# Weight splits moved: ScalarE writes the high halves, VectorE the low halves, GpSimd none

## What is computed

```
def _L0_ffn_ref(hidden_states, gate_w, expert_gate_up, expert_down, shared_gate_up, shared_down, shared_gate_vec):
    ...
    def step(acc, ew):
        w_gu, w_d, cw = ew
        h = _silu_mul(x @ w_gu.T, I)
        return (acc + h @ w_d.T * cw[:, None], None)
    ...
x = x + 0.5 * _L0_ffn_ref(_layernorm(x, axis=-1), ...)
x = x + _L0_attn_ref(_layernorm(x, axis=-1), ...)
x = x + 0.5 * _L0_ffn_ref(_layernorm(x, axis=-1), ...)
x = x + 0.5 * _L1_ffn_ref(_layernorm(x, axis=-1), ...)
x = x + _L1_attn_ref(_layernorm(x, axis=-1), ...)
x = x + 0.5 * _L1_ffn_ref(_layernorm(x, axis=-1), ...)
```

## Time and profile before

| | us |
|---|---|
| median of three runs | 1092.97 |
| lowest, highest | 1092.65, 1095.82 |
| span of the profiled execution | 1092.5 |

### The profile page before, as it was taken

One profiled execution on the slowest core, in us unless ns is written; L12 is line 12 of the kernel. 1 busy time (PEld: TensorE's weight loads), 2 busy tenths in 40 slices (PEclk: granted clock), 3 DMA queues, 4 the chain that ended last, 5 costly groups with the idle time before them and its releaser, 6 DMA issues.

```text
span 1092.5 us, 18432 instructions
## 1 busy us (share of the span) xinstructions
PE 1010.5 (92%) x6692; PEld 584.0 (53%) x6692; DVE 800.6 (73%) x1429; ACT 384.8 (35%) x615; POOL 465.1 (43%) x373
## 2 busy tenths in 40 slices
PE   3989999899899899899799999999999999999997
PEld 1546555455555455555356555554455544555554
DVE  6887776967876967878977786466888778885444
ACT  1223223366423356422232332324432344322332
POOL 3646743466523456525466622231342313422222
PEclk8989999999999999999999999999999999999999
DMA  5212310000000000001233100000000000000000
GB/s 172 87 59 88 101 59 1 1 1 1 1 1 1 1 1 2 1 1 53 64 108 102 44 1 1 0 1 1 1 1 1 1 1 1 1 1 20 1 0 19
DMA packets 11814, 27.38 MB, mean 25 GB/s; under 512 B 1720, under 2 KB 4024, under 8 KB 11744
## 3 DMA queue, kind: packets, MB, share of 16 engines
q1 hardware_dynamic: 11744, 26.44, 8.1%
HBM read 25.38 MB, written 1.05 MB: 24 GB/s over the span
## 4 chain that ended last, share of the span: by engine, by line
PE 51%; DVE 28%; issue 10%; POOL 7%; ACT 3%; DMA 1%; SPq 0%; DVEq 0%; POOLq 0%; ACTq 0%
PE ps L719 28%; PE ps L748 12%; DVE hid L935 4%; POOL hlo L515 3%; DVE hid L937 3%; DVE hid L931 3%; PE ps L730 3%; PE ps L861 2%; POOL scr L554 2%; DVE scr L1119 1%; PE ps L795 1%; PE ps L760 1%; DVE combine L1041 1%; DVE scr L1112 1%; DVE picked L1024 1%
## 5 line engine op out<-in xcount | busy, mean ns | idle before, releaser
L515 POOL TENSOR_TENSOR hlo<-hid,hhi 128x512 f16<-128x512 f32 x208 | 252.2, 1212 | 566.5 <-ACT hhi L592 566.5
L719 PE MATMUL ps<-xhi,whi 128*128 128x512 f16 x832 | 319.7, 384 | 26.1 <-DVE hid L931 25.6
L719 PE MATMUL ps<-xhi,wlo 128*128 128x512 f16 x832 | 319.2, 384 | 0.0
L719 PE MATMUL ps<-xlo,whi 128*128 128x512 f16 x832 | 319.1, 384 | 0.0
L592 ACT ACTIVATE hhi<-hid 128x512 f16<-128x512 f32 x208 | 130.9, 629 | 464.9 <-DVE hid L937 464.7
L931 DVE SCALAR_TENSOR_TENSOR hid<-gtanh,ps 128x512 f32<-128x512 f32 x208 | 142.2, 684 | 174.1 <-ACT gtanh L585 159.6
L748 PE MATMUL ps<-whi,hhi 128*128 128x256 f16 (+1 forms) x832 | 227.7, 274 | 0.8 <-POOL hlo L515 0.8
L748 PE MATMUL ps<-whi,hlo 128*128 128x256 f16 (+1 forms) x832 | 227.3, 273 | 0.0
L748 PE MATMUL ps<-wlo,hhi 128*128 128x256 f16 (+1 forms) x832 | 227.1, 273 | 0.0
L935 DVE TENSOR_TENSOR hid<-hid,ps 128x512 f32<-128x512 f32 x208 | 143.0, 687 | 61.0 <-PE ps L730 56.1
L585 ACT ACTIVATE gtanh<-ps 128x512 f32<-128x512 f32 x208 | 123.3, 593 | 104.7 <-PE ps L719 104.4
(11 more groups left out here) (164 smaller groups left out, 927.4 us busy)
## 6 DMA issues: line engine op xcount, KB each, us to landing
stage<-w_in SPq DMA_DIRECT2D x58, 384.0 KB, 3.1
out<-x SPq DMA_DIRECT2D x2, 512.0 KB, 3.1
sel<-sel_in SPq DMA_DIRECT2D x1, 672.0 KB, 7.7
sel<-sel_in SPq DMA_DIRECT2D x2, 288.0 KB, 3.6
x<-x_in SPq DMA_DIRECT2D x4, 128.0 KB, 2.6
x<-x_in SPq DMA_DIRECT2D x1, 512.0 KB, 8.4
const<-const_in SPq DMA_DIRECT2D x1, 128.0 KB, 2.4
rw<-rw_in SPq DMA_DIRECT2D x1, 64.0 KB, 2.2
```

Of the source, the lines that this page charges most:

```text
L515: pool.tensor_tensor(hlo[:, k, :], hid[:, k % 2, :], hhi[:, k, :], ALU.subtract).then_inc(lo_done, 1)
L719: mm = pe.matmul(ps[:, bank, :], w[:, ds(off, P)], a[:, kc, t0:t0 + HN], start=(n == 0), stop=(n == 3 * KC - 1))
```

## The change

ScalarE now writes `whi`, with one activation that copies `stage` times 256 into f16; VectorE writes `wlo` with one fused operation, `stage` * 256 - `whi`, and waits for ScalarE ahead of it (`w_scaled`). `stage` is no longer written in place. GpSimd has no part in a split. The places in the plan stay: on each engine the split stands behind the chunk's own operations. The waits for the load and, in passes 3 and 4, for the old weights' last use, move from VectorE to ScalarE. SyncE's list and TensorE's stay as they were.

```diff
@@ gpsimd
-            def split(j, g, k):
-                pool.wait_ge(w_scaled, g * 2 + 2)
-                pool.tensor_tensor(wlo[:, ds(j * CW, CW)], stage[:, k, :], whi[:, ds(j * CW, CW)],
-                                   ALU.subtract).then_inc(w_split, 1)
...
-                for j, g, _, slot in splits(r, c, k):
-                    split(j, g, slot)
...
-                elif name == "first_weights":
-                    split(n, n, n)
@@ scalar
+            def split(r, j, group, k):
+                act.wait_ge(stage_loaded[k], group * (16 // SLOTS) + 16)
+                if r in (3, 4):
+                    act.wait_ge(down_done, j + (BASE[3] + 1))
+                act.activation(whi[:, ds(j * CW, CW)], stage[:, k, :], ACT.Copy, scale=W_SCALE).then_inc(w_scaled, 1)
...
                 act.activation(hhi[:, k, :], hid[:, k % 2, :], ACT.Copy).then_inc(hi_done, 1)
+                for j, _, group, slot in splits(r, c, k):
+                    split(r, j, group, slot)
...
+                elif name == "first_weights":
+                    split(PRE, n, 0, n)
@@ vector
-            def split(r, j, g, group, k):
-                dve.wait_ge(stage_loaded[k], group * (16 // SLOTS) + 16)
-                if r in (3, 4):
-                    dve.wait_ge(down_done, j + (BASE[3] + 1))
-                dve.tensor_scalar(whi[:, ds(j * CW, CW)], stage[:, k, :], W_SCALE, None, ALU.mult).then_inc(w_scaled, 1)
-                dve.tensor_scalar(stage[:, k, :], stage[:, k, :], W_SCALE, None, ALU.mult).then_inc(w_scaled, 1)
+            def split(j, g, k):
+                dve.wait_ge(w_scaled, g + 1)
+                dve.scalar_tensor_tensor(out=wlo[:, ds(j * CW, CW)], in0=stage[:, k, :], scalar=W_SCALE,
+                                         in1=whi[:, ds(j * CW, CW)], op0=ALU.mult, op1=ALU.subtract).then_inc(w_split, 1)
```

## The result

The changed kernel takes **1127.31 us** (1127.09 to 1130.03, 4 runs) against 1092.81 us (1090.67 to 1095.82, 4 runs) for the kernel before: ratio 1.031, 95% interval 1.0285 to 1.0335. It is slower by 34.5 us. The forecast was 1126.5 us, with a range of 1107 to 1135. The profiled execution is the slowest of the four (1130.03 us, span 1128.2, mean granted clock 0.984); the spans of the other three are 1125.3 to 1125.6 us at 0.987 to 0.988.

The account below looks back on a forecast made before the run. The prediction took TensorE as the bound at 4.12 us a plain chunk, moving to VectorE's wait loop at 4.76. Terms -1.5 + 6.4 + 8.7 + 7.6 + 11.4 + 0.9 = +33.5 us gave 1126.5 us, range 1107 to 1135.

Parts of the forecast that it names:

- start: Before the first chunks: no GpSimd rival for VectorE, router 0.75 us earlier and 0.7 us less blocking, -1.5 us.
- side work, pass 0: Pass 0 chunks with splits beside layer norm and router: later VectorE queue, partly offset by idle time and less blocking, +6.4 us.
- steady, pass 0: Plain split chunks 12 to 27 of pass 0: 15 x 0.64 us, less 0.9 of slack, +8.7 us.
- +0.9: Loop branches, formerly hidden, delay ScalarE by some 0.1 us every fourth steady chunk: +0.9 us in all.
- side work, pass 3: Pass 3 chunks with splits beside other work, up to chunk 13: hidden product comes later by +7.6 us.
- steady, pass 3 and head of 4: Plain split chunks from chunk 13 of pass 3: 18 x 0.64 us, less 0.9 slack, plus 0.8 residual addition, +11.4 us.
- h: The end of the hidden product's last VectorE operation in a chunk; forecast up to 6.4 us later in pass 0, 7.6 in pass 3.
- rival A: No port wait, hlo and the fused operation run side by side: 4.42 us a plain chunk, 1109 us; chance 0.13.
- The ring: Plain chunks: the loop hhi, whi, wlo, L931, L935, L937 sets the pace at 4.76 us against TensorE's 4.12.
- The port: Plain chunks: the fused operation meets GpSimd's hlo at the shared SBUF port and ends 0.82 us behind it.
- The freed port: Side-work chunks: GpSimd's wlo no longer blocks VectorE, saving 1.5 to 2.3 us in four pass 0 chunks.
- rival C: TensorE's gaps cost clock: the lower level in a fifth of 33 steady chunks, about +23 us, 1150 us; chance 0.05.

Follow-up runs that it names:

- run 2: The changed kernel with GpSimd's hlo waiting, in chunks with a split, until VectorE's fused operation is done: 1121.38 us, ratio 1.026 to the kernel before.
- run 5: The changed kernel with GpSimd's hlo cut to 8 of 512 columns in chunks carrying a split, from the fifth chunk on: 1116.33 us, ratio 1.021 to before.
- run 3: The changed kernel with ScalarE's split gone: VectorE writes whi itself, then the fused low half; GpSimd does no splitting: 1087.95 us, ratio 0.9949 to before.
- Run 1: The changed kernel with ScalarE's whi moved from behind hhi to ahead of the wait for the hidden product: 1077.95 us, ratio 0.9874 to before.

## Why the prediction was right

The last operation of the hidden product (L929) in the changed kernel at five chunks of passes 0, 3 and 4:

```profile
91.09 0.69 DVE L929 SCALAR_TENSOR_TENSOR hid<-hid,ps 128x512 f32<-128x512 f32 x1
...
162.87 0.69 DVE L929 SCALAR_TENSOR_TENSOR hid<-hid,ps 128x512 f32<-128x512 f32 x1
...
510.29 0.69 DVE L929 SCALAR_TENSOR_TENSOR hid<-hid,ps 128x512 f32<-128x512 f32 x1
...
570.84 0.69 DVE L929 SCALAR_TENSOR_TENSOR hid<-hid,ps 128x512 f32<-128x512 f32 x1
...
661.49 0.69 DVE L929 SCALAR_TENSOR_TENSOR hid<-hid,ps 128x512 f32<-128x512 f32 x1
```

They are chunks 12 and 27 of pass 0, 3 and 13 of pass 3 and 4 of pass 4. In the kernel before, the first and the fourth are the earlier trace rows, and the other three are:

```profile
149.16 0.69 DVE L937 SCALAR_TENSOR_TENSOR hid<-hid,ps 128x512 f32<-128x512 f32 x1
...
497.08 0.69 DVE L937 SCALAR_TENSOR_TENSOR hid<-hid,ps 128x512 f32<-128x512 f32 x1
...
629.20 0.69 DVE L937 SCALAR_TENSOR_TENSOR hid<-hid,ps 128x512 f32<-128x512 f32 x1
```

Chunk 0 stands at 22.93 us against 25.77, so each term of the sum can be laid beside its measure, within these two executions:

| term | forecast | measured | from |
|---|---|---|---|
| start | -1.5 | -2.8 | 22.93 - 25.77 |
| side work, pass 0 | +6.4 | +6.6 | 91.09 - 87.36 = 3.7, less the start |
| steady, pass 0 | +8.7 and half of +0.9 | +9.1 | 162.87 - 149.16 = 13.7, less 3.7, less 0.9 of slack taken back in chunk 0 of pass 1 |
| side work, pass 3 | +7.6 | +7.2 | 570.84 - 550.48 = 20.4, less 510.29 - 497.08 = 13.2 |
| steady, pass 3 and head of 4 | +11.4 and half of +0.9 | +11.9 | 661.49 - 629.20 = 32.3, less 20.4 |
| everywhere else | 0 | +3.8 | the rest of 35.7 |

The steps between were right too: of the 21 values that the prediction gives for h in the side-work chunks, none is off by more than 0.4 us in pass 0 and 0.5 in pass 3, once the start and the 13.2 us are taken off. What was luck is that the total came so close: the start gained 1.3 us more than forecast and everywhere else lost 3.8 that were not foreseen, which partly offset each other in this execution, and the other three had spans 2.6 to 2.9 us shorter. In the prediction rival A's 10.2 us should read 33 x 0.3 = 9.9, which moves nothing.

**The ring was right to the hundredth** (4.76 us forecast and measured, and so 0.64 us a chunk) in the chunks like the one shown. In two of four chunks of the loop in pass 0, and in one of four in pass 3, it is 4.84, because hhi starts 0.11 us behind h there and not 0.03. That is what the forecast's +0.9 was for; it came to about 0.5. One part of the ring was wrong without effect: the operation behind ScalarE starts 1.56 us behind h, not 1.43, because of the loop's hand-over. But hlo ends at 102.18 + 1.16 = 103.34, and the operation's end is fixed by that (104.16, 0.82 us behind it), so the later start changed nothing. In all 55 pieces that meet an hlo in the changed kernel the end lies 0.80 to 0.83 us behind it, though the operation arrives 1.42 to 1.65 us behind h. That 0.82 us is what the earlier trace rows had given. The operation runs alone in 0.95 us, as worked out from the earlier trace rows.

**The port** was the step that rested on the fewest rows. Runs 2 and 5 show the contention, and run 3 the same with the roles turned. The rule of the Trainium skill (SBUF — State Buffer, section Who interferes with whom), that a VectorE instruction with two SBUF inputs and a GpSimd instruction that reads SBUF exclude each other and that the order of issue decides who waits, is what all of them show: 1.16 to 1.28 us of the fused operation behind hlo, 0.95 without, and 1.83 us of hlo behind the operation.
What the port is worth was mis-sized in the loop. The prediction said 4.42 us without it; run 2 gives 4.55 to 4.64 there, and 4.42 in written-out chunks alone. The term that was off is the hand-over behind ScalarE, 0.17 us and not 0.03, which shows only when hlo isn't in the way. Rival A at 1109 us would not have come about even with a free port: run 5 has 1116.

**The freed port**, which was to pay for part of the wait in the side-work chunks, did. The four normalisations beside chunk 5 of pass 0 took 1.37 us instead of 3.54, and the router's L1016 in chunk 8 took 0.22 us instead of 1.57:

```profile
50.83 1.28 DVE L911 SCALAR_TENSOR_TENSOR wlo<-stage,whi 128x768 f16<-128x768 f32 x1 [1.43 <-ACT whi L569]
52.04 1.37 DVE L967 TENSOR_SCALAR xn<-x,meanvar,rstd 128x256 f32<-128x256 f32 x4
...
72.70 0.22 DVE L1016 TENSOR_TENSOR picked<-picked,expd 128x64 f32<-128x64 f32 x1
```

Run 1 collects most of the same gain without the price; its four normalisations meet an hlo and take 2.23 us.

**The start** was undersized by 1.3 us. The router's first operation stands at 15.34 us instead of 17.30, and L990 behind it takes 0.23 us instead of 1.12. About 0.6 of the first difference is the fused operation, and 0.9 comes from L990. The remaining 1.3 us are a load: the second piece of weights was there for ScalarE at 12.60, where VectorE had waited until 13.92 in the kernel before. In the six other runs it was there at 12.4 to 13.2 us. So the load was late in the profiled execution of the kernel before, most likely by chance (with one profile of that kernel this isn't shown), and the forecast took it as given.

**Everywhere else** the forecast had nothing, and 3.8 us came. In the stretch where the last router ends and pass 7 begins, the two kernels run the same instructions. The changed kernel, at 1014 to 1026 us in three rows, and then the kernel before, at 980 to 992:

```profile
1014.00:1018.00 4.00, 2.51 (x16) 1.21 (x14) 3.69 (x11) 0.60 (x2) 0.00 (x0) 1.00 0.00 0
1018.00:1022.00 4.00, 2.27 (x9) 1.13 (x10) 2.29 (x4) 1.11 (x3) 1.15 (x1) 0.73 0.00 0
1022.00:1026.00 4.00, 4.00 (x24) 2.20 (x21) 1.38 (x2) 0.65 (x2) 0.43 (x1) 0.84 0.01 2
```

```profile
980.00:984.00 4.00, 2.48 (x16) 1.19 (x13) 3.69 (x11) 0.63 (x2) 0.00 (x0) 1.00 0.00 0
984.00:988.00 4.00, 2.31 (x16) 1.43 (x17) 2.52 (x5) 1.08 (x2) 1.15 (x1) 1.00 0.00 0
988.00:992.00 4.00, 4.00 (x26) 2.34 (x25) 1.94 (x4) 1.23 (x2) 1.16 (x1) 1.00 0.00 0
```

TensorE is busy 2.5 of 4 us in both and then 2.3; in one execution the granted clock falls to 0.73 in this row and 0.84 in the next, in the other it stays. By these rows 4 x 0.27 + 4 x 0.16 = 1.7 us of clock are lost, and h loses 1.7 us there. The changed kernel's execution has two of them behind chunk 4 of pass 4 that the kernel before doesn't have, which is the +3.4 there. The other 0.4 is what is left of falls that only one of the two had between passes 0 and 3. Of rival C's mechanism this much is true: where TensorE has gaps, the granted clock falls in some executions. The changed kernel also had a fall in the side work of pass 3 (0.72 from 554 to 560 us) that the kernel before had not; VectorE set the pace there, and h's steps in those chunks were no longer than forecast. But in the steady stretches of 4.76 us, with gaps in every chunk, the granted clock was 1.00, so the rival did not happen where it was placed.

## What to carry to other kernels

Moving work to an idle engine takes load off, and can still lengthen the ring that sets the pace: count the cycle through the new wait (here 1.4 to 1.6 us to the other engine's result, behind everything queued there), not the busy time. If two halves of a job go to two engines, let the first half be done in the idle time of its engine ahead of the work both wait for, or let the second half lag by one turn: two moved lines made 1127 us into 1078 us. And where a two-input operation on VectorE meets GpSimd reading SBUF, one of them stands still, so ask which of the two has someone waiting.

## What the hardware showed beyond that

- The port is given by order of arrival, and the VectorE operation that waits ends 0.80 to 0.83 us (768 columns) or 0.55 us (512) behind GpSimd's, a little less than its own duration (0.95 and 0.68). The other way round, in run 3, hlo ended at 111.87 + 1.83 = 113.70, 1.01 us behind the fused operation, and takes 1.16 alone.
- In a loop whose waits and addresses are computed, an operation of VectorE starts 0.14 to 0.17 us behind ScalarE's end, against 0.03 us in code that is written out. A price taken from written-out chunks is too low for a loop.
- The same instructions, with nearly the same gaps, kept their granted clock in the execution of one kernel and lost it in that of the other, at 1.7 us a fall. Some 3 us of 1100 can come and go that way, so a difference of a few us between two profiles should be laid beside the granted clock before it is given a cause.
- The first loads' arrival differs by over a microsecond between the profiled executions (12.4 to 13.9 us for the second piece of weights), and at the start all of it was on the path.
